# The shared expert's nine-tap convolution by five products for three outputs, with a new order of the lanes and of early preparations

## The chip, the cores and the metric

The kernel runs on one core of one Trainium2 chip. The metric is the device time of one execution in microseconds (us), the median of several runs. In the names of the profile PE is TensorE (PEld its weight loads), DVE VectorE, ACT ScalarE, POOL GpSimd and SP SyncE, which issues DMAs.

## What is computed

An audio tower on x of 8 batches of 750 tokens with 128 channels in float32: layer 0 has a convolution mixer, a gated recurrence and a mixture of 8 experts with a shared one; layer 1 a linear attention over 8 heads and a mixture of 10 experts with a shared convolution. After the mixer's pooling 748 tokens a batch are left. The part that the change rewrites is the shared convolution of layer 1:

```python
xt = jnp.transpose(x, (0, 2, 1))
...
sh = conv1d_same(xt, sh_w1, sh_b1)     # 128 -> 512 channels, 9 taps
sh = jax.nn.silu(sh)
sh = conv1d_same(sh, sh_w2, sh_b2)     # 512 -> 128 channels, 1 tap
sh = jnp.transpose(sh, (0, 2, 1))
z = residual + y + sh
```

## The kernel before

Each engine has one straight program; semaphores order them, and an engine that waits holds back all that stands behind. The phases are: the mixer of layer 0, its experts, attention with the shared convolution, the experts of layer 1 (208 tiles of rows), and the output sums. Between phases stand barriers.

Attention goes over four pairs of batches (ITERS = 4, LANES = 2). A lane has 25 steps: step 0 and 1 sum the experts' rows, take variance 5 and norm 5 on VectorE (rstd 5 on GpSimd between them), step 2 is norm5T on TensorE, 3 to 7 the projections q0, q1, k0, k1 and v, 8 to 19 six chunks of scores and context, 20 (OUT_STEP) the output projection, 21 norm6T, 22 and 23 the router's convolutions, 24 its scores. `interleaved` (from line 579) writes out the order that all engines share: after each step of a lane it puts in as many parts of the convolution of the pair before (i - 1) as the weights FILL allow. Attention of pair 0 has none of them (`conv` is False); after pair 3 its convolution stands alone, the tail.

The convolution (PARTS, line 549 on; `conv_part` on three engines) takes nine taps as three groups g of three. A half-batch q (375 or so columns) and a quarter m of the 512 channels are one unit. With the minimal form for two outputs and three taps it needs four products a, b, c, d of 192 or 182 columns each for a group, into two PSUM banks, "bc" and "ad", 12 instructions a product pair (a float32 matmul is two instructions). ScalarE copies each bank out (line 1434), VectorE combines (`conv_combine`, lines 2015 to 2019), ScalarE takes silu (1422), TensorE then multiplies four quarters with conv2 for three tiles of tokens ("rows", line 1142), ScalarE copies (1447, 1448) and GpSimd adds them to N (`add_conv_rows`, 2199 to 2203). Rows of half-batch q stand after the first product pair of unit (q + 1, m = 1), and those of half-batch 3 at the end (CONV_END).

GpSimd's program for a pair (`attention`, from line 2228) is: turn(1, i-1), rstd 5 of both lanes (2111), add_b_out, add_b_v, add_b_sh2(1, i-1), scatter of lane 0's rows (12 indirect DMAs, 2130), add_conv_rows(0), scatter of lane 1, add_conv_rows(1), rstd 6 of both lanes, add_conv_rows(2), turn(0, i), add_b_sh2(0, i), add_conv_rows(3). `turn` (2225 to 2227) makes the inputs of the products from the transposed norm 6; `add_b_sh2` adds one bias to N and ln_b to H (2191, 2193); `make_conv_weights` (2209 to 2213) stands in pair 0 only. Its memory for the products is `wreg`; the turned inputs lie in NT.

## Time and profile before

| | us |
|---|---|
| median of 3 runs | 1531.79 (1531.74 to 1535.3) |
| the profiled execution | 1544.43 |
| its span | 1542.6 |
| busy TensorE, VectorE, GpSimd, ScalarE | 1305.9, 1003.6, 699.3, 644.9 |
| attention of pair 0, without convolution | 582.0 to 686.6 |
| pairs 1, 2, 3 | 686.6 to 857.0, to 1022.0, to 1186.6 |
| the tail | 1186.6 to 1267.6 |
| experts of layer 1, output | to 1480, to 1542 |

Times of rows count from the start of the span. A row of the order of time has the start, the length of the merged group, engine, line, operation, what it writes and reads, count, and in brackets how long the engine had been idle and what ended that. The granted clock (PEclk) is a share of 2.4 GHz; 0.50 is TensorE's lower level of 1.2 GHz.

### The profile page before, as it was taken

To read this page: it belongs to the slowest core of one execution; us is meant where nothing else is said; L and a number is where in the kernel's file an instruction comes from. 1 tells how busy PE (TensorE), PEld (TensorE's weight loads), DVE (VectorE), ACT (ScalarE), POOL (GpSimd) and SP (SyncE) were. 2 spreads that over 40 slices of the span, in tenths; PEclk is the share of its full clock that TensorE was granted. 3 is DMA by queue.
4 is the path that set the end of the run, shared out by engine and by line. 5 is a ranking of instruction groups with operands and counts; after the bars stand their busy time and mean duration, and the time that the engine had idled before them with its cause. 6 is when DMAs were issued, how large, how long until landed. Compare 5 with 4: busy or idle time off the path is not lost.

```text
span 1542.6 us, 33397 instructions
## 1 busy us (share of the span) xinstructions
PE 1305.9 (85%) x10360; PEld 1103.2 (72%) x10361; DVE 1003.6 (65%) x3235; ACT 644.9 (42%) x1610; POOL 699.3 (45%) x1055
## 2 busy tenths in 40 slices
PE   6696777787899937778899899988998989999974
PEld 3464646564899935556788778876887989999953
DVE  4467768665466656757863786467663628989946
ACT  1346272523122204335335453445334436666623
POOL 0112556444688853133531444242614526777732
PEclk9697989898999978989999899999998999999987
DMA  6000400003588840010010001000100237777725
GB/s 191 4 21 6 111 27 22 25 21 95 161 266 256 263 170 1 2 42 1 24 61 0 2 14 58 14 1 1 43 1 8 95 97 191 196 194 198 196 88 161
DMA packets 102202, 128.46 MB, mean 83 GB/s; under 512 B 21015, under 2 KB 61181, under 8 KB 101842
## 3 DMA queue, kind: packets, MB, share of 16 engines
q1 hardware_dynamic: 88786, 102.36, 23.1%
q0 software_dynamic: 13312, 24.74, 4.8%
q8 instruction: 62, 1.02, 0.3%
q14 instruction: 42, 0.34, 0.1%
HBM read 96.13 MB, written 34.94 MB: 85 GB/s over the span
## 4 chain that ended last, share of the span: by engine, by line
PE 60%; DVE 15%; issue 7%; DVEq 6%; POOL 5%; ACT 4%; DMA 2%; POOLq 0%; SPq 0%; ACTq 0%
PE psum L980 12%; PE psum L1133 11%; PE psum L989 9%; DVE work L1554 3%; PE psum L1142 3%; PE psum L1047 2%; POOL rows_in L2130 2%; PE psum L1094 2%; PE psum L1072 2%; PE psum L794 2%; PE psum L1191 2%; PE psum L969 2%; PE psum L1018 2%; DVE stats L1537 2%; PE psum L1067 1%
## 5 line engine op out<-in xcount | busy, mean ns | idle before, releaser
L1133 PE MATMUL psum<-NT,wreg 128*128 128x182 f32 (+1 forms) x1536 | 261.6, 326 | 10.2 <-ACT pack L1434 5.1
L1133 PEld LDWEIGHTS psum<-NT,wreg 128*128 128x128 f32 x1536 | 247.9, 192 | 18.9 <-ACT pack L1434 5.9
L2162 POOL DMA_INDIRECT rows_out<-work,expert_row_kept x208 | 206.2, 992 | 79.6 <-issue 41.1
L980 PE MATMUL psum<-work 128*128 128x128 f32 x1664 | 222.7, 277 | 0.9 <-ACT work L1336 0.9
L980 PEld LDWEIGHTS psum<-work 128*128 128x128 f32 x1664 | 203.9, 193 | 1.7 <-issue 0.9
L2111 POOL TENSOR_TENSOR rstd<-var_eps,pack 128x6 f32<-128x6 f32 x40 | 56.5, 1415 | 215.0 <-DVE var_eps L1544 214.9
L1329 ACT ACTIVATE work<-psum,work 128x128 f32<-128x128 f32 x416 | 118.6, 368 | 64.4 <-PE psum L980 64.3
L1876 DVE SCALAR_TENSOR_TENSOR work<-psum,work 128x128 f32<-128x128 f32 x416 | 117.1, 344 | 7.7
L794 PE MATMUL psum<-pack,work 128*128 128x128 f32 (+2 forms) x288 | 51.4, 336 | 82.0 <-DVE work L1554 75.5
L1885 DVE TENSOR_SCALAR work<-psum,expert_row_kept 128x128 f32<-128x128 f32 x208 | 72.8, 350 | 71.8 <-PE psum L969 36.6
L2130 POOL DMA_INDIRECT rows_in<-N,slot_now x96 | 100.5, 1046 | 28.6 <-issue 28.4
L989 PE MATMUL psum<-work 128*128 x832 | 110.2, 275 | 1.4 <-DVE work L1876 1.4
L794 PEld LDWEIGHTS psum<-pack,work 128*128 128x128 f32 (+2 forms) x288 | 42.2, 176 | 91.4 <-DVE work L1554 57.3
L989 PEld LDWEIGHTS psum<-work 128*128 128x128 f32 x832 | 101.2, 192 | 2.0 <-issue 2.0
L1322 ACT ACTIVATE work<-psum 128x256 f32<-128x256 f32 x104 | 39.9, 383 | 124.1 <-PE psum L980 116.6
L1047 PE MATMUL psum<-work 64*128 64x256 f32 (+1 forms) x384 | 56.5, 414 | 17.6 <-DVE work L1961 14.7
L1934 DVE TENSOR_TENSOR work<-psum,pack 128x1024 f32<-128x1024 f32 (+1 forms) x48 | 56.5, 1192 | 21.9 <-PE psum L1049 20.6
L1142 PE MATMUL psum<-wreg,conv_h 128*128 128x128 f32 (+1 forms) x384 | 55.4, 311 | 14.5 <-ACT conv_h L1422 14.5
L2199 POOL TENSOR_TENSOR slots_seen<-pack 128x1 f32<-128x1 f32 x16 | 3.1, 191 | 140.5 <-ACT conv_rows L1448 129.5
L969 PE MATMUL psum<-pack,work 128*128 128x128 f32 x208 | 58.7, 283 | 8.2 <-DMA work<-rows_in 5.6
L1142 PEld LDWEIGHTS psum<-wreg,conv_h 128*128 128x128 f32 (+1 forms) x384 | 53.7, 222 | 15.0 <-ACT conv_h L1422 15.0
L989 PE MATMUL psum<-wreg,work 128*128 x416 | 63.6, 276 | 0.8 <-DVE work L1864 0.8
(364 smaller groups left out, 2894.3 us busy)
## 6 DMA issues: line engine op xcount, KB each, us to landing
work<-w_and_b SPq DMA_DIRECT2D x104, 258.0 KB
work<-in_ew SPq DMA_DIRECT2D x104, 256.0 KB
work<-rows_in SPq DMA_DIRECT2D x208, 65.0 KB
work<-rows_out SPq DMA_DIRECT2D x32, 384.0 KB, 4.2
rows_out<-work,expert_row_kept POOLq DMA_INDIRECT x208
work<-in_xT SPq DMA_DIRECT2D x8, 375.0 KB, 3.0
w_and_b<-in_ew SPq DMA_DIRECT2D x1, 2560.0 KB
out<-H SPq DMA_DIRECT2D x8, 320.0 KB
```

The source lines that it names most:

```text
L794: r = nc.tensor.transpose((acc or v.P)[:, j // 3, c0:c0 + widths[j]], src(j), ident[0:widths[j], 0:widths[j]])
L969: nc.tensor.transpose(v.psx, v.x, ident).then_inc(pe_done[k], pe.step(phase, "xT", k))
L980: r_ = mm(v.ps1[:, c * P:(c + 1) * P], v.w1[:, c * P:(c + 1) * P], v.xT, start=True, stop=True)
L989: r_ = mm(v.psy, v.e[:, c * P:(c + 1) * P], weights[:, bass.ds(which[u] * nh + c * P, P)], start=(c == 0), stop=(m == 0 and c == nh - 1))
L1047: mm(acc[:, :, 0:n], v.QK[2 + g][rows, col], v.QB[rows, g, :, 0:n], start=True, stop=True)
L1133: r = mm(bank[:, half * HALF_PAIRS:half * HALF_PAIRS + p1 - p0], weights[:, m * P:(m + 1) * P], product_input(name, g, k, p0, p1), start=( ...
L1142: r = mm(acc, conv_h[:, m, j * P:j * P + n_], conv2[:, m * P:(m + 1) * P], start=(m == 0), stop=(m == 3))
L1329: r_ = A(v.e[:, c * P:(c + 1) * P], v.ps1[:, c * P:(c + 1) * P], ACT.Exp, bias=v.b1[:, c:c + 1])
L1876: r_ = V.scalar_tensor_tensor(v.e[:, cols], v.ps1[:, cols], v.b1[:, c:c + 1], v.e[:, cols], ALU.add, ALU.max)
L1885: V.tensor_scalar(v.y, v.psy, v.gate, None, ALU.mult).then_inc(dve_done[k], dve.step(phase, "y", k))
L2130: G.indirect_dma_start(rows_in[m], bass.IndirectOffsetOnAxis(ap=slot_now[0:n, q, j:j + 1], axis=0), staged(m, q, k)[0:n, j % TILES, :], No ...
L2162: G.indirect_dma_start(rows_out[m], bass.IndirectOffsetOnAxis(ap=v.dest, axis=0), v.y, None, bounds_check=last, oob_is_err=False).then_inc ...
```

## The change

The convolution takes the minimal form for three outputs and three taps: five products (points 0, 1, 2, 3, 4) of 250 columns over a whole batch k, in fills p12, p03 (12 instructions each) and p4 (6), alternating between two banks. A unit is now a batch and a quarter m, eight in a pair in place of sixteen. The weights of two points are made on GpSimd, in eight adds of 1536 columns where there were three; `turn` makes the five inputs in one add of 504 and eleven of 252 columns with three drains between, in place of three of 754. VectorE combines in seven instructions of 250 columns. The quarters m = 2, 3 of the silu input lie in the first two batches of H, which are stored to DRAM before and loaded back during the experts of layer 1; copies of p03 and p4 have one buffer, those of p12 two. Rows of half-batches 0 and 1 come after unit (1, 0), those of 2 and 3 both at the end. ln_b's add is a step of its own (`add_ln_b`), for both lanes right behind turn(0). `interleaved` spreads the parts by COST; without convolution lane 1 goes a step behind lane 0 from step 2 to 7. On VectorE variance 5 and norm 5 of lane 1 are one step, and the router's taps and the route's constants are made before it waits for the row stores. GpSimd's order of steps is not changed otherwise.

```diff
+TRIPLES = (L + 2) // 3
+TURNED = TRIPLES + 2
...
+        CONV_POINTS = 5
+        conv_w = wreg[:, 0:CONV_POINTS * 3 * 512].rearrange("p (x g c) -> p x g c", x=CONV_POINTS, g=3)
+        conv2 = wreg[:, CONV_POINTS * 3 * 512:CONV_POINTS * 3 * 512 + 512]
...
+        conv_h_own = sb("conv_h", [P, 2, TILES * P])
+        conv_h = [conv_h_own[:, m, :] for m in range(2)] + [
+            H[:, m * TILES:(m + 1) * TILES, :].rearrange("p j d -> p (j d)") for m in range(2)]
+        first_rows = H[:, 0:LANES * TILES, :].rearrange("p j d -> p (j d)")
...
+        conv_sum = NTf[:, SUM_AT:SUM_AT + TRIPLES]
+        conv_p12 = [pack[:, PACK[at][0]:PACK[at][0] + 2 * TRIPLES] for at in ("compress", "Wg")]
+        conv_p034 = sb("conv_p034", [P, 3 * TRIPLES])
+        conv_p03, conv_p4 = conv_p034[:, 0:2 * TRIPLES], conv_p034[:, 2 * TRIPLES:]
...
-        UNIT = [(q, m) for q in range(UNITS) for m in range(4)]
+        UNIT = [(k, m) for k in range(LANES) for m in range(4)]
+        POINTS = {"p12": (1, 2), "p03": (0, 3), "p4": (4,)}
 
 
         PARTS = []
-        for u, (q, m) in enumerate(UNIT):
-            PARTS.append(("bc", q, m))
-            if m == 1 and q > 0:
-                PARTS.append(("rows", q - 1, 0))
-            PARTS.append(("ad", q, m))
-        CONV_END = [("last", UNITS - 1, 3), ("rows", UNITS - 1, 0)]
+        for k, m in UNIT:
+            PARTS += [(x, k, m) for x in POINTS]
+            if m == 0 and k > 0:
+                PARTS += [("rows", 2 * k - 2, 0), ("rows", 2 * k - 1, 0)]
+        CONV_END = [("last", LANES - 1, 3), ("rows", UNITS - 2, 0), ("rows", UNITS - 1, 0)]
+        COST = {"p12": 6, "p03": 6, "p4": 3, "rows": 4}
+        FILLS = [f"{x}{m}_{k}" for x, k, m in PARTS + CONV_END if x != "last"]
...
+            costs = [COST[x] for x, *_ in PARTS]
+            turns_ = [(x // LANES, x % LANES) for x in range(ATT_STEPS * LANES)]
+            if not conv:
+                ahead = [x for x in turns_ if x[0] < CHUNKS]
+                ahead.sort(key=lambda x: (x[0] + (x[1] if x[0] > 1 else 0), x[1]))
+                turns_ = ahead + turns_[len(ahead):]
+            for step, lane_ in turns_:
+                order.append(("attention", step, lane_))
+                reached += FILL[step]
+                while conv and n < len(PARTS) and sum(costs[:n]) * sum(FILL) * LANES < reached * sum(costs):
                     order.append(("conv", n, 0))
                     n += 1
...
+            for t, x in enumerate((0, 1, 4)):
+                sp.dma_start(conv_w[:, x], d["conv1"].rearrange("p (g t c) -> p g t c", g=3, t=3)[:, :, t, :]).then_inc(conv_in, 16)
+            sp.dma_start(conv2, d["conv2"]).then_inc(conv_in, 16)
...
+            sp.wait_ge(first_rows_final, 1)
+            sp.dma_start(first_rows_dram, first_rows).then_inc(first_rows_out, 16)
...
+            sp.wait_ge(pe_conv_done, pe_conv.end("conv")[0][1])
+            sp.wait_ge(first_rows_out, 16)
+            sp.dma_start(first_rows, first_rows_dram).then_inc(first_rows_back, 16)
...
+                fill = f"{what}{m}_{k}"
+                bank = fill_bank(fill)
+                before, bi = fill_before(fill, i)
+                e.wait_ge(act_conv_done, act_conv.at("conv", before, 0, bi))
...
+                    if what == "p12" and m == 0:
                         e.wait_ge(pool_done[k], pool.at("attention", "turned", k, i))
-                    e.wait_ge(act_conv_done, act_conv.at("conv", f"{what}{bm}_{bq}", 0, bi))
-                    if what == "ad" and m == 1 and q > 0:
-                        e.wait_ge(act_conv_done, act_conv.at("conv", f"rows{q - 1}", 0, i))
-                    elif what == "ad" and m == 0 and q == 0:
...
+                bk, bm, bi = unit_before(k, m, i, 2 if what == "p12" else 1)
+                e.wait_ge(dve_conv_done, dve_conv.at("conv", f"y{bm}_{bk}", 0, bi))
+                dst = {"p12": conv_p12[u % 2], "p03": conv_p03, "p4": conv_p4}[what]
+                nc.scalar.copy(dst, bank[:, 0:len(POINTS[what]) * TRIPLES]).then_inc(act_conv_done, act_conv.step("conv", fill, 0))
+                if what == "p03" and u > 0:
+                    conv_silu(*UNIT[u - 1], i)
...
             def second_step(k, i):
-                (norm5 if k == 0 else var5)(k, i)
-
-            def third_step(k, i):
                 if k > 0:
-                    norm5(k, i)
-
-            att = {0: [begin_lane], 1: [second_step], 2: [third_step]}
+                    var5(k, i)
+                norm5(k, i)
+
+            att = {0: [begin_lane], 1: [second_step]}
...
+                if u == 2:
+                    e.wait_ge(first_rows_out, 16)
+                e.wait_ge(act_conv_done, act_conv.at("conv", f"p4{m}_{k}", 0, i))
+                V.scalar_tensor_tensor(conv_sum, p1, 3.0, p2, ALU.mult, ALU.add)
+                V.scalar_tensor_tensor(p2, p1, -3.0, p2, ALU.mult, ALU.add)
+                V.scalar_tensor_tensor(p0, p0, 3.0, p3, ALU.mult, ALU.add)
+                V.scalar_tensor_tensor(conv_p4, conv_p4, 1.5, p3, ALU.mult, ALU.add)
                 e.drain()
-                V.scalar_tensor_tensor(y[:, 0], conv_sum[:, 0:n_], 0.5, a, ALU.mult, ALU.add)
-                V.scalar_tensor_tensor(y[:, 1], b, 0.5, d_, ALU.mult, ALU.subtract
-                                       ).then_inc(dve_conv_done, dve_conv.step("conv", f"y{m}_{q}", 0))
+                V.tensor_tensor(y[:, 0], p0, conv_sum, ALU.subtract)
+                V.scalar_tensor_tensor(y[:, 1], p3, 2.0, p2, ALU.mult, ALU.add)
+                V.scalar_tensor_tensor(y[:, 2], conv_p4, 4.0, conv_sum, ALU.mult, ALU.subtract
+                                       ).then_inc(dve_conv_done, dve_conv.step("conv", f"y{m}_{k}", 0))
...
+            def add_ln_b(k, i, first):
+                e.drain()
+                e.wait_ge(dve_done[k], dve.at("attention", "norm6", k, i))
+                G.tensor_tensor(slots_seen[:], w("nought"), w("nought"), ALU.add)
                 for h, n, tiles in tile_halves(H[:, batch_tiles(i * LANES + k), :]):
-                    G.tensor_tensor(h, h, w("ln_b")[0:n].unsqueeze(1).broadcast_to([n, tiles, P]), ALU.add)
+                    r = G.tensor_tensor(h, h, w("ln_b")[0:n].unsqueeze(1).broadcast_to([n, tiles, P]), ALU.add)
+                if first and k == LANES - 1:
+                    r.then_inc(first_rows_final, 1)
...
+                s = N[:, LANES * TILES:2 * LANES * TILES, :].rearrange("p j d -> p (j d)").rearrange("p (g c) -> p g c", g=3)
+                w0, w1, w2, w3, w4 = (conv_w[:, x] for x in range(CONV_POINTS))
+                e.wait_ge(conv_in, 64)
+                G.tensor_tensor(s, w0, w4, ALU.add)
+                G.tensor_tensor(w3, w1, w1, ALU.add)
                 e.drain()
-                G.tensor_tensor(conv_c, s, conv_taps[:, :, 1], ALU.subtract)
+                G.tensor_tensor(w2, s, w1, ALU.subtract)
+                G.tensor_tensor(w3, w3, w0, ALU.add)
                 e.drain()
-                G.tensor_tensor(conv_taps[:, :, 1], conv_taps[:, :, 1], s, ALU.add)
+                G.tensor_tensor(w1, w1, s, ALU.add)
+                e.drain()
+                G.tensor_tensor(s, w4, w4, ALU.add)
+                e.drain()
+                G.tensor_tensor(s, s, s, ALU.add)
+                e.drain()
+                G.tensor_tensor(w3, w3, s, ALU.add)
                 e.drain().then_inc(conv_made, 1)
...
+                    v = NTf[:, at:at + 3 * TURNED].rearrange("p (r s) -> p s r", s=3)
+                    return v[:, 0:n] if n > 1 else v[:, 0]
+
+                G.tensor_tensor(t[:, 3:5], x(3, 2), x(1, 2), ALU.subtract)
+                G.tensor_tensor(t[:, 0], x(0), x(2), ALU.subtract)
+                G.tensor_tensor(t[:, 1], x(1), x(2), ALU.add)
+                G.tensor_tensor(t[:, 2], x(1), x(2), ALU.subtract)
+                e.drain()
+                G.tensor_tensor(t[:, 0], t[:, 0], t[:, 0], ALU.add)
+                G.tensor_tensor(t[:, 1], t[:, 3], t[:, 1], ALU.subtract)
+                G.tensor_tensor(t[:, 2], t[:, 2], t[:, 2], ALU.add)
+                G.tensor_tensor(t[:, 4], t[:, 4], t[:, 3], ALU.subtract)
+                e.drain()
+                G.tensor_tensor(t[:, 0], t[:, 0], t[:, 3], ALU.add)
+                G.tensor_tensor(t[:, 2], t[:, 2], x(3), ALU.add)
+                G.tensor_tensor(t[:, 4], t[:, 4], t[:, 3], ALU.subtract)
+                e.drain()
+                G.tensor_tensor(t[:, 2], t[:, 2], x(2), ALU.subtract
                                 ).then_inc(pool_done[k], pool.step("attention", "turned", k))
...
                 if not first:
                     add_conv_rows(2, i - 1)
                 turn(0, i)
+                add_ln_b(0, i, first)
+                add_ln_b(1, i, first)
                 add_b_sh2(0, i)
                 if not first:
                     add_conv_rows(3, i - 1)
```

## Rows read from the trace of the kernel before

**Rows 1.** The stretches, each engine's busy time and TensorE's granted clock.

```profile
core 0: us, PE busy (x) PEld busy (x) DVE busy (x) ACT busy (x) POOL busy (x), PEclk, DMA share, GB/s
...
857.00:1022.00 165.00, 152.66 (x1372) 128.76 (x1373) 106.59 (x297) 77.08 (x172) 61.66 (x71) 0.96 0.06 21
```

**Rows 2.** The same stretches, the convolution's matmuls of line 1133 alone.

```profile
857.00:1022.00 165.00, 66.18 (x392) 62.18 (x393) 0.96 0.06 21
...
1186.60:1267.60 81.00, 62.58 (x384) 61.16 (x384) 0.97 0.29 93
```

**Rows 3.** TensorE in order of time, the tail after the last batch pair.

```profile
1193.28 15.68 PE L1133 MATMUL psum<-NT,wreg 128*128 128x192 f32 x96
1208.80 2.84 PE L1142 MATMUL psum<-wreg,conv_h 128*128 128x128 f32 x24
...
1262.19 4.56 PE L1142 MATMUL psum<-wreg,conv_h 128*128 128x128 f32 x24 [2.56 <-ACT conv_h L1422]
```

**Rows 4.** TensorE in order of time, from one out projection past the boundary.

```profile
798.16 1.60 PE L1086 MATMUL psum<-pack,work 128*128 128x128 f32 x12
799.60 2.82 PE L1142 MATMUL psum<-wreg,conv_h 128*128 128x128 f32 x24
...
816.52 0.86 PE L794 MATMUL psum<-pack,work 128*128 128x128 f32 x6
...
851.41 5.27 PE L1142 MATMUL psum<-wreg,conv_h 128*128 128x128 f32 x24 [3.98 <-ACT conv_h L1422]
...
857.20 15.87 PE L1133 MATMUL psum<-NT,wreg 128*128 128x192 f32 x96 [0.51 <-issue]
...
877.29 9.66 PE L1018 MATMUL psum<-work,pack 128*128 128x384 f32 x24
```

**Rows 5.** GpSimd in order of time, first conv rows, scatter, rstd6 of pair 1.

```profile
766.93 0.19 POOL L2199 TENSOR_TENSOR slots_seen<-pack 128x1 f32<-128x1 f32 x1 [2.09 <-issue]
...
768.39 0.33 POOL L2125 TENSOR_TENSOR slots_seen<-pack 128x1 f32<-128x1 f32 x1 [0.17 <-issue]
769.09 0.99 POOL L2130 DMA_INDIRECT rows_in<-wreg,slot_now  x1 [0.37 <-issue]
...
783.24 0.99 POOL L2130 DMA_INDIRECT rows_in<-work,slot_now  x1 [0.30 <-issue]
...
804.71 1.47 POOL L2111 TENSOR_TENSOR rstd<-var_eps,pack 128x6 f32<-128x6 f32 x1
```

**Rows 6.** GpSimd in order of time, at the boundary between two pairs.

```profile
848.55 2.21 POOL L2191 TENSOR_TENSOR N<-N,row_bias 128x640 f32 x2 [17.17 <-ACT work L1403]
850.73 1.68 POOL L2193 TENSOR_TENSOR H<-H,pack 128x640 f32 x2
...
859.45 1.44 POOL L2225 TENSOR_TENSOR NT<-NT 128x754 f32<-128x754 f32 x1
```

**Rows 7.** GpSimd in order of time, the weights' preparation in pair 0.

```profile
618.05 3.45 POOL L2211 TENSOR_TENSOR wreg<-conv_h,wreg 128x1536 f32<-128x1536 f32 x1 [8.64 <-issue]
621.65 3.41 POOL L2213 TENSOR_TENSOR wreg<-wreg,conv_h 128x1536 f32<-128x1536 f32 x1 [0.15 <-issue]
```

**Rows 8.** VectorE in order of time, pair 0 and the start of pair 1.

```profile
565.95 1.02 DVE L1895 MEMSET work<- 128x1152 f32 x1 [9.66 <-DMA rows_out<-work,expert_row_kept]
...
621.85 3.36 DVE L1957 TENSOR_TENSOR work<-work,upd 128x128 f32<-128x128 f32 x1
...
688.20 8.21 DVE L1916 TENSOR_TENSOR H<-work,H 128x640 f32 x2 [0.20 <-issue]
...
704.59 1.63 DVE L1554 TENSOR_SCALAR work<-H,mean_var,rstd 128x128 f32 x6 [0.18 <-issue]
...
709.73 2.99 DVE L1554 TENSOR_SCALAR work<-H,mean_var,rstd 128x128 f32 x6 [0.25 <-POOL rstd L2111]
```

**Rows 9.** TensorE in order of time, pair 0.

```profile
585.51 1.51 PE L794 MATMUL psum<-pack,work 128*128 128x128 f32 x6 [4.85 <-DVE work L1554]
...
626.59 2.08 PE L1047 MATMUL psum<-work 64*128 64x256 f32 x8 [5.77 <-DVE work L1961]
```

More of the change, by code:

```diff
@@ L1145, in none @@
+                r.then_inc(pe_conv_done, pe_conv.step("conv", fill, 0))
             def none(k, i):
@@ new lines, in conv_silu @@
+            def conv_silu(k, m, i):
+                e.wait_ge(dve_conv_done, dve_conv.at("conv", f"y{m}_{k}", 0, i))
+                A(conv_h[m][:, 0:L], conv_h[m][:, 0:L], ACT.Silu, bias=w("b_sh1", (m, m + 1)), scale=1.0 / 6.0
+                  ).then_inc(act_conv_done, act_conv.step("conv", f"s{m}_{k}", 0))
+            def conv_part(n, i):
+                what, k, m = (PARTS + CONV_END)[n]
+                u = 4 * k + m
+                if what == "last":
+                    conv_silu(k, m, i)
+                    return
+                fill = f"{what}{m}_{k}"
+                bank = fill_bank(fill)
+                e.wait_ge(pe_conv_done, pe_conv.at("conv", fill, 0, i))
+                if what == "rows":
+                    q = k
@@ L2021, in conv_combine @@
                 e.drain()
             def conv_part(n, i):
[L2024 to L2027 removed]
+                what, k, m = (PARTS + CONV_END)[n]
+                if what == "p12" and 4 * k + m > 0:
+                    conv_combine(*UNIT[4 * k + m - 1], i)
                 elif what == "last":
[L2029 removed]
+                    conv_combine(k, m, i)
```

190 lines of the change are left out of this document (75 added, 115 removed).

## The prediction

> **Names.** Eight batches run in pairs: pair 0 to pair 3 of the attention loop, two lanes (0 and 1) in a pair. A pair's convolution is done while the next pair's attention runs; that of the last pair is the tail. Rows_q are the pointwise products of half-batch q (24 instructions of line 1142), a fill is one group of convolution products between two bank changes. All engines run their programs in order.
>
> **What bounds the kernel now.** I read the stretches first, then TensorE's own order of time, then GpSimd's. In a pair's stretch of 165.0 us TensorE is busy 152.7, VectorE 106.6, GpSimd 61.7 [rows 1]: TensorE is the bound, and 66.2 us of it are the products of line 1133, 62.6 in the tail [rows 2]. So work taken from TensorE there is worth its length, as long as nothing else comes late. The reader is to see a second thing: GpSimd is idle most of the time, but it is one queue, and TensorE waits through it: for rstd (line 2111), for the turned inputs (2225 to 2227). What stands ahead of these in GpSimd's program matters, not its busy share.
>
> **The gain on TensorE.** Per pair the old form needs 384 instructions of 192 or 182 columns (two for each matmul call), the new one 2 batches x 4 m x 15 calls x 2 = 240 of 250 columns. 96 old ones took 15.68 us, 0.163 each, and 24 of 128 columns 2.84, 0.118 [rows 3]. Through both points 250 columns cost 0.204, in proportion to columns 0.212; I take 0.212, since 0.163 for 192 is nearly in proportion. A pair is then 50.9 us against 62.6, or 54 against 66 at a pair's mean clock: **12 us less** in each of four places, 47 in all. Against this stands the order of the work.
>
> **First wait: rstd6 behind the scatter.** Counting the fills of `interleaved` with the new costs (8 units of 15 plus 8, total 128): at step OUT_STEP of lane 0 the fraction reached is 25.5/39 or 83.7, so rows_0 and rows_1 (ending at 79 and 83) come only right after out of lane 0; before, rows_0 came in chunk 1 and only rows_1 stood there, at 799.60 [rows 4]. GpSimd's program is unchanged there: rows_0, scatter of lane 1, rows_1, rstd6. Before, that scatter ran from 769.09 to 784.23 and was over when rows_1 came [rows 5]. Now it starts after rows_0. From rows_0's end on TensorE to norm6 of lane 0: ScalarE's copy 0.7, the add 1.5 (766.93 to 768.39), to the first issue 0.7, twelve issues 15.1, the gap behind them 2.1, rows_1 1.5, rstd 1.5 [rows 5], norm6 1.6 [rows 8]: 24.7 us. TensorE has beside it rows_1 2.8, three fills of 2.5, 2.5 and 1.3, and out of lane 1 1.5 [rows 3, 4]: 10.7. **It waits 14 us**, in pairs 1 to 3, and stands before norm6T (816.52 in pair 1 [rows 4]).
>
> **Second wait: the turned inputs behind rows_2.** Rows_2 moves from inside the pair to its end (CONV_END), behind the last silu, and GpSimd adds it before `turn(0)`. Before, turn(0) was long done when the pair ended. Now the next pair's first fill waits for: copy 0.7, the add 1.5, turn. Turn is new too: one add of 504 and eleven of 252 columns and three drains in place of three of 754 at 1.44 [rows 6]. By that row's 1.91 ns a column it is 6.3 + 0.5 = 6.8 us; by 2.25 ns of the 1536-column adds (3.45 [rows 7]) and the 0.19 that one column costs [rows 5] 10.2. I take 8.5. So the first fill starts 11 us after rows_2's end; rows_3 (2.8 to 5.3) is all that lies beside it.
>
> **Third wait: rstd5 behind two turns.** After turn(0) GpSimd has add_ln_b twice (1.68 and a gate each, 2.1; before one of them stood here, now both do), b_sh2 2.2 [rows 6], rows_3 1.5, turn(1) 8.5, rstd5 1.5. With the 11 that is 28.9 us after rows_2's end, 30.6 with norm5 of lane 0. The fills ahead of it are 54 instructions, 11.4 us, done at about 24 with the slow clock below. From the start of norm5 of lane 0 to the end of that of lane 1 the kernel before takes 8.1 us (704.59 to 712.72 [rows 8]); only now there is no fill between. So q0 starts 5.3 (rows_2) + 38.5 = 43.8 us after rows_2's start, where before it was 877.29 - 851.41 = 25.9 after rows_3's start [rows 4], with 96 of 384 instructions done against 54 of 240.
>
> **A cycle of pairs 2 and 3**, from the last rows' start: q0 at 43.8. From q0 to out of lane 0 the old cycle has 165.0 - 79.1 = 85.9 us [rows 1, 4]; the fills in it fall from 132 instructions at 0.172 (66.2/384 [rows 2]), 22.7, and one rows group to 96 at 0.212, 20.4, of which I count 4 of the 5 us, since VectorE's combine grows from four to seven instructions. Out at 125.7, rows_0's end at 130.0, norm6T at 154.7. From norm6T to the last rows the old pair has 34.9 us with 84 instructions (14.2), one rows group (2.8) and 4.0 idle [rows 4]; the new one 60 instructions (12.7), no rows group, 4.7 idle for the longer combine and silu and 2.5 for the clock: 33.8. The cycle is 188.5, **23.6 over** the 164.9 of before, twice: **+47.2**.
>
> **The clock.** After 4.0 us without work rows_3 took 5.27 for what is 2.82 at the full clock [rows 4]: TensorE ran at the lower of its two levels, 1.2 in place of 2.4 GHz. Each new long gap costs about 2.5 so; I put it behind the two gaps above and in the tail, and one more rows group lies at the end.
>
> **Pair 1.** At its start no rows stand before the turns. Turn(1) and b_sh2 lie as before and the longer turn ends about where the old one with ln_b did, so q0 is taken as before (2 less to 3 more). Then -4 in the chunks, 24.7 + 4.3 from out to norm6T in place of 18.4 [rows 4], 33.8 in place of 34.9: **+5.6**.
>
> **The tail** from rows_2's start: 5.3 + 11 + 50.9 + two rows groups 5.7 + 3 (clock; one late combine behind the slots) + 4.7 idle + rows_2 and rows_3 8.5 (24 took 4.56 in the old tail [rows 3]) = 89.1; before 5.3 + 80.2 (1186.6 to 1266.8 [rows 2, 3]): **+3.7**. The scatter ends at about 71 and the first expert rows come before TensorE is free, so the later scatter costs nothing; it would cost its excess over 18 us. The 8-unit order needs turn(1) at 44 us, it ends at 33.
>
> **Pair 0.** The weights' preparation grows from three adds of 1536 columns to eight, 3.4 us each [rows 7]. While one ran, a 0.29 us add of VectorE took 3.36 and ended with it, and TensorE stood 5.77 [rows 8, 9]. The old three cost about 7 us (three VectorE instructions stretched so), in proportion the five new ones 12; I take +12, with the bounds +4 (most of them meet nothing) and 5 x 3.4 = +17 (each holds VectorE for its whole length). The Trainium skill, "SBUF — State Buffer", section "Who interferes with whom", states that a VectorE instruction with two SBUF inputs and a GpSimd instruction that reads SBUF exclude each other for a whole instruction. By it the upper bound would hold wherever VectorE has such an instruction next, and the longer turns would hold it back too, so the rule speaks against this change; the trace agrees for the one add (621.85 + 3.36 against 621.65 + 3.41). VectorE's preparations before the row stores: it waited 9.66 there [rows 8], so they are hidden, but the loads of Y land about as late: -1.5 (0 to -2.2). The step between lanes: TensorE was idle 4.85 before norm5T of lane 1 [rows 9], but lane 1's chain starts no sooner: -1.5 (0 to -4.9). Sum **+9**. The store and reload of first rows (768 KB) run on SP's queue beside compute; it stands ahead of loads due a pair later, and is over before combine 2 asks: 0.
>
> **Sum.** 9 + 5.6 + 47.2 + 3.7 = +65.5 on the profiled execution of 1544.4. That is 0.8% above the median of the runs, so +65 on 1531.8: **1597 us**.
>
> **Rivals.** (a) The forecast, 0.68. (b) VectorE and GpSimd block each other more: combine 0 and h3 fall into turn(1) (two adds took 8.21 us beside GpSimd [rows 8]), 4 us a boundary, weights at +17: +15, 1612; for it speaks that the boundary now has 25 us of GpSimd without a pause; 0.12. (c) Small turns are cheap, 4.3 us as the old: two turns less a cycle and one in the tail, 4.2 x 5 = -21: 1576; against it speak the fixed part of each instruction and the drains; 0.10. (d) Faster: TensorE's columns alone decide. -47, +9 for pair 0, +12 for rows at the lower clock and longer ends: 1506. It decides if norm6 follows rows_0 within 10.7 us and turn(0) rows_2 within 5; twelve issues alone are 15.1, so I give it 0.06. (e) The waits and the gain cancel, within 0.3%: 0.04 (a measurement of this kernel can tell 0.3% from no change).
>
> **Range and chances.** (a) spans 1570 to 1622 by its bounds: pair 0 +3 to +15, turns 6.8 to 10.2 in five places. The range 1565 to 1625 takes in (c) and (b). Faster 0.06, same 0.04, slower 0.90.
>
> **What would show it.** TensorE idle about 14 us before line 794's norm6T, released by VectorE, with GpSimd's twelve issues between the first two adds of conv rows; the first fill released by GpSimd's turn, 11 us after rows_2; norm5T late by 5 to 10 us; conv matmuls of 0.21 us and four groups of about 52 us; adds of 1536 columns x8 in pair 0. A granted clock below 0.95 in pairs 2 and 3. Wrong would be: rstd6 ahead of the scatter, or turn under 5 us.

## The result, and the profile after

| | before | changed |
|---|---|---|
| median, us | 1532.2 (1531.7 to 1535.3, 4 runs) | 1619.1 (1612.5 to 1623.4, 4 runs) |
| profiled execution, its span | 1544.4, 1542.6 | 1612.5, 1610.5 |
| ratio of the times | 1 | 1.056 [1.051, 1.061] |
| busy TensorE, VectorE, GpSimd | 1305.9, 1003.6, 699.3 | 1266.6, 997.0, 749.8 |

The changed kernel is 87 us slower. The direction is as forecast (1597, range 1565 to 1625), and the time is 22 us above the predicted time. TensorE is busy 39 us less and the kernel takes longer, so the loss is all waiting. TensorE's waits in the changed kernel (line waited in, what released it; total, times, longest):

```profile
PE psum L827 <- DVE work L1586: 140.6, 22, 24.5
PE psum L1174 <- POOL NT L2289: 26.8, 3, 9.4
...
PE psum L1167 <- ACT H L1454: 18.8, 5, 4.7
```

Line 827 is the transposes (794 before), 1174 the convolution (1133), 1167 the rows (1142), 2289 the last instruction of the turn. The same pair in TensorE's order of time, beside [rows 4]:

```profile
859.58 1.23 PE L1167 MATMUL psum<-wreg,conv_h 128*128 128x128 f32 x4 [4.74 <-ACT H L1454]
...
876.23 13.57 PE L1174 MATMUL psum<-NT,wreg 128*128 128x250 f32 x54 [9.39 <-POOL NT L2289]
896.17 1.51 PE L827 MATMUL psum<-pack,work 128*128 128x128 f32 x6 [6.37 <-DVE work L1586]
902.59 1.51 PE L827 MATMUL psum<-pack,work 128*128 128x128 f32 x6 [4.91 <-DVE work L1586]
...
1016.91 1.51 PE L827 MATMUL psum<-pack,work 128*128 128x128 f32 x6 [14.37 <-DVE work L1586]
...
1050.61 1.22 PE L1167 MATMUL psum<-wreg,conv_h 128*128 128x128 f32 x4 [4.74 <-ACT H L1454]
```

From one pair's last rows to the next pair's are 191.0 us, where before there were 163.6 and 166.3. In them TensorE is idle 48.1 us (12.3 before): the first fill waits for the turn, norm5T for both lanes' norms, norm6T for rstd6. GpSimd at the same boundary, to be read beside [rows 6]:

```profile
864.91 0.19 POOL L2239 TENSOR_TENSOR slots_seen<-pack 128x1 f32<-128x1 f32 x1 [39.19 <-ACT conv_rows L1472]
...
866.15 1.03 POOL L2275 TENSOR_TENSOR NT<-NT 128x504 f32<-128x504 f32 x1
...
875.40 0.78 POOL L2289 TENSOR_TENSOR NT<-NT 128x252 f32<-128x252 f32 x1
876.40 0.19 POOL L2229 TENSOR_TENSOR slots_seen<-pack 128x1 f32<-128x1 f32 x1 [0.22 <-issue]
...
882.34 0.19 POOL L2239 TENSOR_TENSOR slots_seen<-pack 128x1 f32<-128x1 f32 x1 [0.21 <-issue]
...
883.58 1.04 POOL L2275 TENSOR_TENSOR NT<-NT 128x504 f32<-128x504 f32 x1
...
893.12 1.33 POOL L2144 TENSOR_TENSOR rstd<-var_eps,pack 128x6 f32<-128x6 f32 x1
```

GpSimd stood idle 39 us waiting for rows_2, while turn(0)'s inputs were complete from 828.5 on (ScalarE's copy of norm6T), 36 us earlier, and then worked 29.5 us almost without a pause, with rstd5 at the end of it. The row with 39.19 in brackets is the cause of the wait for the turn. The cause of the wait at norm6T is in GpSimd's rows between the adds of rows_0 and rows_1, to be read beside [rows 5]:

```profile
992.96 0.19 POOL L2239 TENSOR_TENSOR slots_seen<-pack 128x1 f32<-128x1 f32 x1 [35.11 <-ACT conv_rows L1472]
...
995.12 1.18 POOL L2163 DMA_INDIRECT rows_in<-NT,slot_now  x1 [0.52 <-issue]
...
1012.60 0.19 POOL L2239 TENSOR_TENSOR slots_seen<-pack 128x1 f32<-128x1 f32 x1 [2.16 <-issue]
...
1013.83 2.66 POOL L2144 TENSOR_TENSOR rstd<-var_eps,pack 128x6 f32<-128x6 f32 x2
```

The twelve issues stand between the two adds, and both rstd6 behind them; VectorE had waited 13.15 us for them when it began norm6.

### The profile page after: what moved, and what is told of

The parts are those of the page before. It is cut to its first block, busy times and chain, and to the rows that moved or that the text cites. A ratio compares the mean times of both kernels' runs of the same rounds, so it can differ in the third digit from the quotient of the medians.

```text
span 1610.5 us, 32139 instructions
## 1 busy us (share of the span) xinstructions
PE 1266.6 (79%) x9784; PEld 1042.6 (65%) x9785; DVE 997.0 (62%) x3204; ACT 620.0 (38%) x1540; POOL 749.8 (47%) x1140
## 3 DMA queue, kind: packets, MB, share of 16 engines
q1 hardware_dynamic: 90130, 103.93, 22.7%
## 4 chain that ended last, share of the span: by engine, by line
PE 40%; issue 22%; DVE 13%; POOL 12%; ACT 4%; DVEq 3%; POOLq 3%; DMA 2%; SPq 0%; ACTq 0%
PE psum L1013 11%; PE psum L1022 8%; POOL rows_in L2163 6%; PE psum L1174 4%; DVE work L1586 2%; PE psum L1224 2%; PE psum L1002 2%; PE psum L827 2%; PE psum L1051 1%; POOL rstd L2144 1%; DVE stats L1569 1%; PE psum L845 1%; PE psum L1080 1%; PE psum L846 1%; POOLq L2237 1%
## 5 line engine op out<-in xcount | busy, mean ns | idle before, releaser
L1174 PE MATMUL psum<-NT,wreg 128*128 128x250 f32 x960 | 224.9, 390 | 30.2 <-POOL NT L2289 26.8
L1174 PEld LDWEIGHTS psum<-NT,wreg 128*128 128x128 f32 x960 | 186.6, 199 | 56.6 <-POOL NT L2289 19.1
L827 PE MATMUL psum<-pack,work 128*128 128x128 f32 (+2 forms) x288 | 56.9, 361 | 146.9 <-DVE work L1586 140.6
L827 PEld LDWEIGHTS psum<-pack,work 128*128 128x128 f32 (+2 forms) x288 | 46.7, 191 | 158.5 <-DVE work L1586 124.1
L1022 PE MATMUL psum<-work 128*128 x832 | 110.2, 275 | 1.8 <-DVE work L1908 1.8
L2045 DVE SCALAR_TENSOR_TENSOR NT<-pack 128x250 f32<-128x250 f32 x32 | 15.6, 487 | 104.1 <-ACT conv_p L1478 94.1
L1586 DVE TENSOR_SCALAR work<-H,mean_var,rstd 128x128 f32 (+1 forms) x96 | 31.4, 397 | 51.4 <-POOL rstd L2144 50.8
```

What stands on the lines that cost most here:

```text
L827: r = nc.tensor.transpose((acc or v.P)[:, j // 3, c0:c0 + widths[j]], src(j), ident[0:widths[j], 0:widths[j]])
L1022: r_ = mm(v.psy, v.e[:, c * P:(c + 1) * P], weights[:, bass.ds(which[u] * nh + c * P, P)], start=(c == 0), stop=(m == 0 and c == nh - 1))
L1174: r = mm(bank[:, half * TRIPLES:(half + 1) * TRIPLES], conv_w[:, x, g, k_cols(m)], turned(k)[:, x, g:g + TRIPLES], start=(g == 0), stop=(g ...
```

## The experiments

All times of one table row come from one chip, and each ratio is to the kernel before on that chip, since the chips differ. "Cycle" is the time from the last rows of pair 1 to those of pair 3, halved, read in the trace. The kernel before has one trace only, that of its profile above; its cycle does not come from the group on A. On which chip the first comparison ran is not known; the changed kernel was not run again on A or B.

| kernel | chip | median | ratio to before | cycle |
|---|---|---|---|---|
| before | A | 1533.0 | 1 | 164.9 (trace of its profile) |
| changed (first comparison, before 1532.2) | | 1619.1 | 1.056 [1.051, 1.061] | 191.1 |
| e1: rows_2 behind turn(0) | A | 1588.0 | 1.037 [1.033, 1.041] | 181.8 |
| e2: rstd6 ahead of the rows | A | 1583.1 | 1.034 [1.030, 1.038] | 181.1 |
| e3: both | A | 1559.2 | 1.016 [1.012, 1.020] | 172.4 |
| e4: both, rstd5 ahead of turn(1) | A | 1570.9 | 1.023 [1.019, 1.027] | 176.1 |
| before | B | 1667.3 | 1 | |
| e5: both, turn(0) behind norm6 | B | 1660.3 | 0.996 [0.993, 0.998] | 188.4 |
| e6: changed, three weights' adds | B | 1704.9 | 1.025 [1.021, 1.029] | 207.0 |
| e7: before with the small parts | B | 1681.4 | 1.009 [1.006, 1.012] | 193.1 |
| e8: before with a long turn | B | 1692.2 | 1.013 [1.010, 1.017] | 193.9 |
| before | C | 1652.7 | 1 | |
| e9: changed | C | 1698.6 | 1.028 [1.023, 1.033] | 206.5 |
| e10: as e3 | C | 1671.4 | 1.011 [1.006, 1.016] | 196.2 |
| e11: as e5 | C | 1644.8 | 0.994 [0.990, 0.997] | 187.7 |
| e12: e5 and norm5 ahead | C | 1628.1 | 0.986 [0.982, 0.990] | 180.5 |

### Are the two waits in GpSimd's queue the loss? (e1, e2, e3)

e1 changes the end of GpSimd's `attention`, e2 its middle:

```diff
-                if not first:
-                    add_conv_rows(2, i - 1)
                 turn(0, i)
                 add_ln_b(0, i, first)
                 add_ln_b(1, i, first)
                 add_b_sh2(0, i)
                 if not first:
+                    add_conv_rows(2, i - 1)
                     add_conv_rows(3, i - 1)
```

```diff
                     scatter(1, i - 1, [0])
-                    add_conv_rows(0, i - 1)
                     scatter(1, i - 1, [1])
-                    add_conv_rows(1, i - 1)
                 for k in range(LANES):
                     rstd("attention", 6, k, i)
+                if not first:
+                    add_conv_rows(0, i - 1)
+                    add_conv_rows(1, i - 1)
```

> The changed kernel, with GpSimd's add of the third convolution rows (add_conv_rows(2)) moved behind turn(0), both add_ln_b and add_b_sh2(0), just ahead of add_conv_rows(3). Same instructions on every engine, only GpSimd's order differs. Theory (GpSimd's queue at the boundary of the pairs): turn(0) no longer waits for TensorE's third rows, so the 9.4 us wait of the first fill goes in pairs 1 to 2 and in the tail (8.1 us), and norm5 of the next pair starts some 8 to 10 us sooner, since turn(0), ln_b and b_sh2(0) are done ahead of the rows: 2 x 14 to 18 + 8 = 36 to 44 us less than the changed kernel, about 1578 against 1619. Rival 1 (VectorE and GpSimd stand in each other's way, and that is the cost): the same work overlaps, so less than 10 us go. Rival 2 (the order hides a third wait that takes its place, norm5's rstd behind turn(1)): only the fill's 27 us go.

> The changed kernel, with GpSimd's rstd6 of both lanes moved ahead of add_conv_rows(0) and (1), and the second half of the scatter ahead of them too; nothing else differs. Theory (rstd6 behind the scatter behind the first rows): TensorE's wait of 14.4 us at norm6 in each of pairs 1 to 3 goes, 43 us less in all, about 1576 against 1619; what is next late is VectorE's own norm6, some 3 us of each may stay, so 34 to 43. Rival 1 (contention of VectorE and GpSimd): under 10 us go. Rival 2 (the scatter itself, 12 indirect DMA a lane at about 1.3 us each, is what rstd6 waits for, not the rows): half of it stays.

> Both moves of GpSimd's queue together, nothing else. Theory: the two waits are in different places of a pair and add up: 36 to 44 and 34 to 43 us, so 70 to 87 less than the changed kernel, 1532 to 1549, about the kernel before. Rival (the convolution's work is in part the cover of what follows, or contention is the cost): less than 50 us go, above 1569.

Measured against the changed kernel's 1619: -31, -36 and -60 us, each good to about 9 us. The 1619 come from the first comparison and not from the group on A, but the kernel before took 1532.2 there and 1533.0 on A; on chip C, where the changed kernel and the one with both moves ran together (e9, e10), the two moves give back 27 of 46 us. Both rivals of pure contention (under 10 us) fall: with not one instruction changed, an order gives back 60 of the 87 us. The cycles add up: -9.3, -10.0, together -18.7. e1's 31 lie between the 27 of its rival 2 and the 36 of the theory. The third wait did not take the place of the first, as that rival had it: from the last rows to q0 are 13.6 us less, and norm5T of lane 0 waits 0.2 in place of 6.4 in pair 2; but 3.1 are lost again between norm6T and the next last rows. e1's waits, in the form of the first list, no longer hold the one for the turn, and the tail, which waited for its first turn too, is 12.3 us shorter (85.0 to 72.7 to the start of the last rows). The line for the silu grew by 4.5; turn(0) and add_b_sh2(0) now lie beside the last combine:

```profile
PE psum L827 <- DVE work L1586: 133.6, 24, 25.0
PE psum L1080 <- DVE work L1998: 25.5, 18, 6.6
PE psum L1167 <- ACT H L1454: 23.3, 5, 6.3
```

e2's line for the norms fell from 140.6 to 106.8, 11 us a pair, and not 14: norm6T still waits 1.1 and 2.2 for VectorE. Both scatters still stand ahead of rstd6, so they were not the reason by themselves, as rival 2 of e2 had it: they cost only where the second started behind rows_0. In e3 the norms' line stands at 107.8, but one wait at norm6T is back:

```profile
991.76 0.86 PE L827 MATMUL psum<-pack,work 128*128 128x128 f32 x6 [1.10 <-DVE work L1586]
...
1001.04 1.51 PE L827 MATMUL psum<-pack,work 128*128 128x128 f32 x6 [5.87 <-DVE work L1586]
```

e1 and e3 came out under what was expected and e2 near its lower end: each time a part of the gain met the next wait.

### The third wait (e4)

```diff
-                if not first:
-                    turn(1, i - 1)
                 for k in range(LANES):
                     rstd("attention", 5, k, i)
+                if not first:
+                    turn(1, i - 1)
```

> Both moves, and the third wait as well: GpSimd does rstd5 of both lanes ahead of turn(1) at the start of a pair (the turned columns get a semaphore of their own so that this order can be said). Theory: norm5 of lane 0 no longer waits for turn(1)'s 9.6 us where that is not already covered: 5 to 10 us less in each of pairs 1 to 3 beside the two moves, 15 to 30 in all: 1505 to 1530, at or below the kernel before (1532). Rival: norm5 then waits for VectorE's var5 behind its combine of the convolution, and nothing more goes (within 5 us of the kernel with both moves).

The rival is right, and worse than it said: 12 us slower than e3 in the median (four runs each, 1561.9 to 1572.8 against 1552.6 to 1565.1), and 3.7 in the cycle. GpSimd gives rstd5 sooner, but VectorE's program has the first combine of the convolution ahead of norm5, and it waits for ScalarE's copy of p4. In e3 already:

```profile
878.66 0.49 DVE L2045 SCALAR_TENSOR_TENSOR NT<-pack 128x250 f32<-128x250 f32 x1 [7.65 <-ACT conv_p L1478]
...
882.74 1.63 DVE L1586 TENSOR_SCALAR work<-H,mean_var,rstd 128x128 f32 x6 [0.18 <-issue]
```

In e3 turn(1) lay beside these 7.65 us of an idle VectorE. In e4 GpSimd stands still there instead, for var5 of lane 1, which VectorE does behind the combine and norm5 of lane 0. Turn(1) then comes from 885.2 to 893.9, and add_b_out behind it beside the route's count, whose first copy takes 1.26 us where it takes 0.22 in e3:

```profile
883.90 1.33 POOL L2148 TENSOR_TENSOR rstd<-var_eps,pack 128x6 f32<-128x6 f32 x1 [11.42 <-DVE var_eps L1578]
885.20 1.03 POOL L2279 TENSOR_TENSOR NT<-NT 128x504 f32<-128x504 f32 x1
...
893.89 4.59 POOL L2213 TENSOR_TENSOR H<-H,row_bias 128x640 f32 x4
```

TensorE has a new wait there (9.1 us over three pairs), and from norm5T to norm6T of lane 1 are 115.2 us in place of 110.2:

```profile
PE psum L938 <- DVE N L1710: 9.1, 3, 3.4
```

### Contention of VectorE and GpSimd (e5, e11)

```diff
                 else:
+                    add_b_sh2(0, i - 1)
                     add_b_sh2(1, i - 1)
...
                 for k in range(LANES):
                     rstd("attention", 6, k, i)
+                add_ln_b(1, i, first)
+                add_ln_b(0, i, first)
                 if not first:
                     add_conv_rows(0, i - 1)
                     add_conv_rows(1, i - 1)
                 turn(0, i)
-                add_ln_b(0, i, first)
-                add_ln_b(1, i, first)
-                add_b_sh2(0, i)
```

> The kernel with both moves, and GpSimd's order changed once more, with no instruction added or taken: add_ln_b(1) and add_ln_b(0) (which wait for norm6) go ahead of the adds of the first two rows and of turn(0), and add_b_sh2(0) goes to the next pair, beside add_b_sh2(1). In the trace of the kernel with both moves norm6 of lane 1 took 5.81 us for six instructions beside turn(0), where six alone took 1.63. Theory of contention between VectorE and GpSimd: with GpSimd idle there those six take about 1.6 again, TensorE's 5.87 us wait at norm6 of lane 1 falls to about 1.7, and the last combine ahead of the last rows loses some 1.3: 4 to 6 us a pair, 12 to 18 in all: 1541 to 1547 against 1559. Rival (what bounds there is something else, the six are only stretched because nobody waits for them): no difference beyond 3 us.

> The kernel whose turn(0) waits until norm6 of lane 1 is over, again, now beside the kernel with both moves. Its trace has all of norm6's instructions at 0.33 to 0.35 us, where up to 3.19 us stood beside the turn. Theory of contention: 0.008 to 0.012 below the ratio of the kernel with both moves (12 to 18 us). Rival (the stretched instructions lay in slack): within 0.003 of it, and the gain seen came from the chip.

The six instructions of norm6 of lane 1 in e3, beside turn(0), and in e5, with GpSimd idle:

```profile
995.17 5.81 DVE L1586 TENSOR_SCALAR work<-H,mean_var,rstd 128x128 f32 x6
```

```profile
1067.41 1.63 DVE L1586 TENSOR_SCALAR work<-H,mean_var,rstd 128x128 f32 x6
```

TensorE's wait behind them falls from 5.87 to 0.94, and that for the silu ahead of the last rows from 6.25 to 4.74. e5 ran on chip B, where e3 did not, so its whole time decides nothing. On chip C, where both ran, e11 is 0.017 below e10, 27 us, with intervals that do not touch. The slack theory falls. The size is larger than the 12 to 18 expected. The two cycles give 8.5 each, 17.0, and norm5T to the last rows in pair 1 another 7.9. At the end of pair 0, where turn(1) had stood behind both add_ln_b and add_b_sh2(0), come about 5 more: norm5T of lane 1 is 8.3 us earlier, of which 3.3 were there when attention began. Since add_b_sh2(0) and add_ln_b were moved too, the whole 27 us is not contention's: the two waits above are 6.4 us a pair (the six instructions alone 4.2), and what the moved adds bring by themselves no run took apart.

### Pair 0 and the small parts (e6, e7)

e6 makes three adds in `make_conv_weights` and leaves out five, so its output differs. e7 puts into the kernel before this, and VectorE's early preparations:

```diff
+            if not conv:
+                ahead = [x for x in turns_ if x[0] < CHUNKS]
+                ahead.sort(key=lambda x: (x[0] + (x[1] if x[0] > 1 else 0), x[1]))
+                turns_ = ahead + turns_[len(ahead):]
...
-                (norm5 if k == 0 else var5)(k, i)
+                if k > 0:
+                    var5(k, i)
+                norm5(k, i)
```

> The changed kernel with three of the eight adds that make the convolution's weights (the kernel before had three); the other weights are left out, so the output differs, and nothing else does. Theory: pair 0 is longer by these adds, each about 3 us of GpSimd beside VectorE's work, which stretches VectorE's instructions: 6 to 12 us less than the changed kernel, 1607 to 1613 against 1619. Rival (they lie in idle time): no difference; and the 6 us by which pair 0 grew come from elsewhere.

> The kernel before with the two small parts of the change alone: lane 1 a step behind lane 0 up to the first chunks in pair 0, and VectorE's early preparations with var5 and norm5 of lane 1 in one step. No new convolution. Theory of the sum: 3 us less in pair 0 (1.5 and 1.5), nothing elsewhere: 1528 to 1532 against 1533. Rival 1 (the merged step puts norm5 of lane 1 directly behind its own variance, with rstd5's round trip through GpSimd uncovered): 2 to 3 us more in each pair, 1537 to 1541. Rival 2: nothing that can be measured.

The whole time of e6 can't be set beside the changed kernel's, which ran on another chip (1.025 against 1.028 on C). Its trace can: from norm5T of lane 0 to norm6T in pair 0 are 91.0 us in e6, 97.0 in e9, 96.9 in the changed kernel's first trace and 90.0 in that of before. So five adds are 6.0 us, 1.2 each, and not the 12 of the forecast; the gain is at the lower end of the 6 to 12 expected, and the rival falls.

e7 came out 15 us slower than before (10 to 20), where 3 less were forecast. Pair 0 gained nothing: 90.6 us in that stretch against 90.3 in e8, which has the old step order, and the wait before it 22.7 against 22.9. What the traces show of the loss is at the start of pairs 1 to 3, where q0's first product now waits:

```profile
939.76 1.51 PE L799 MATMUL psum<-pack,work 128*128 128x128 f32 x6 [2.94 <-DVE work L1559]
943.81 2.86 PE L1023 MATMUL psum<-work,pack 128*128 128x384 f32 x4 [2.54 <-ACT work L1360]
```

In [rows 4] q0 follows norm5T without a wait. So it does in e8, on the same chip and with the old steps. The three such waits (3.2, 2.5 and 2.9) are 8.7 us; for the rest of the 15 there is no trace of before on chip B, and it stays open. Rival 1 had the place right and the size at half.

### The turn's length alone (e8)

```diff
+                for again in range(2):
+                    G.tensor_tensor(t[:, 0, :, 0:n], x(0), x(2), ALU.subtract)
+                    G.tensor_tensor(t[:, 1, :, 0:n], x(1), x(2), ALU.add)
+                    G.tensor_tensor(t[:, 2, :, 0:n], x(2), x(1), ALU.subtract)
+                    e.drain()
```

> The kernel before with a turn of eight instructions instead of three (the first three repeated and repeated again in part, with the same results), about 11.5 us instead of 4.3; the convolution is the old one. Theory (queue): turn(0) stays hidden, since in this kernel only the last rows stand at the pair's end and turn(0) is not behind them; turn(1) holds rstd5 back, so norm5 of lane 0 comes about 5 us later at each boundary: 10 to 20 us more, 1543 to 1553. That is far from the 87 us of the whole change: what costs is the order in which the rows, the turn and rstd stand, not the turn's length. Rival (the turn's work beside VectorE costs by itself): 7 us twice a pair, 30 us or more.

Measured +22 us (16 to 28), just above the theory's 10 to 20 and under the rival's 30. The turn has nine instructions, not the eight that I had counted, and took 14.6 us beside VectorE's work (930.77 to 945.41), so turn(1) is 10 longer, twice the 4 to 6 by which the change lengthens it. The 22 us cannot be set beside the 87, since the kernel before took 1532 us in that comparison and 1667 on B: on B the changed kernel without five of its adds (e6) is 42 us slower than before, so about 48 with them. Halved for the shorter turn, e8 leaves it some 11 us of that, an estimate: a longer turn costs some, and the 9.3 and 10.0 us a cycle that e1 and e2 gave back by order alone are more. The trace shows what the turn does to VectorE:

```profile
930.82 4.22 DVE L1544 TENSOR_SCALAR var_eps<-mean_var 128x6 f32<-128x6 f32 x1
...
936.09 3.24 DVE L1916 TENSOR_TENSOR H<-work,H 128x640 f32 x2 [0.20 <-issue]
```

The first takes 0.17 and the second 1.03 with GpSimd idle.

### A version that beats both (e9, e10, e12)

e12 takes e5, puts rstd5 ahead of turn(1) as e4, and clears VectorE's way too (the separate wait in norm5_kept stands for what the combine had implied, that ScalarE has read norm 6):

```diff
-        FILL = [3, 1, 0, 0, 0, 0, 1, 0] + [0.5, 0.5] * TILES + [3.5, 2, 1.5, 1, 0.5]
+        FILL = [2, 0, 2, 0, 0, 0, 1, 0] + [0.5, 0.5] * TILES + [3.5, 2, 1.5, 1, 0.5]
...
                 add_experts(k, i)
-                if k == 0:
-                    var5(k, i)
+                var5(k, i)
...
-            att = {0: [begin_lane], 1: [second_step]}
+            def norm5_kept(k, i):
+                e.wait_ge(act_done[k], act.at("attention", "kept", k, i - 1))
+                norm5(k, i)
+
+            att = {0: [begin_lane], 1: [norm5_kept]}
```

> The changed kernel itself once more, as the reference of this group on one chip, since the chip of the last group gave the kernel before 1667 us where the chip of the group before it gave 1533. Expected from its first comparison: 1.056 times the kernel before on a chip like the first. On a chip like the second, where TensorE stands idle at many single instructions with nothing awaited, the changed kernel has 576 TensorE instructions fewer, so the ratio may be lower, 1.03 to 1.05.

> The kernel with both moves of GpSimd's queue again, beside the next one on the same chip. Expected: 1.016 times the kernel before on a chip like the first, and 0.035 to 0.045 below the changed kernel's ratio on any chip, since the two waits do not depend on it.

> The same, and the pair's boundary in another order on VectorE and GpSimd: var5 of both lanes in the first step, norm5 of both lanes in the second, with fewer of the convolution's fills ahead of them and more behind norm5's transposes (2, 0, 2 in place of 3, 1, 0 of the planner's dues), so that no combine stands ahead of norm5; GpSimd's rstd5 of both lanes goes ahead of turn(1). Theory (after the queue's waits and the contention, what is left over the kernel before is norm5 behind the first combine, with a 5.6 us wait of TensorE at norm5 of lane 1 and 1 at lane 0): 5 to 7 us a pair less, 15 to 21 in all, so the ratio falls by another 0.010 to 0.014, to 0.99 or below. Rival 1 (as rstd5 ahead of turn(1) alone brought nothing and cost 12: turn(1) then stands beside VectorE's work of the first chunks): no gain or a loss. Rival 2 (the fills that came ahead of norm5 were its cover): TensorE waits at norm5 of lane 0 instead, and half of the gain stays.

e12 is 1.4% faster than the kernel before and 4.2% faster than the changed one on the same chip. Its boundary has no wait at norm5T:

```profile
897.36 1.22 PE L1169 MATMUL psum<-wreg,conv_h 128*128 128x128 f32 x4 [4.74 <-ACT H L1456]
...
907.85 6.59 PE L1176 MATMUL psum<-NT,wreg 128*128 128x250 f32 x30 [2.11 <-issue]
914.28 0.81 PE L829 MATMUL psum<-pack,work 128*128 128x128 f32 x6
914.92 2.71 PE L1176 MATMUL psum<-NT,wreg 128*128 128x250 f32 x12
917.47 0.80 PE L829 MATMUL psum<-pack,work 128*128 128x128 f32 x6
```

What cost 3.7 us a cycle alone in e4 brings 7.2 with its partner on VectorE. That both engines on the way to norm5 had to be cleared at once is argued: VectorE's new order was not run with GpSimd's old one. The ratio fell by 0.008, a little less than the 0.010 to 0.014 expected.

e9 fell as expected or a little more (1.028, where 1.03 to 1.05 stood), but e10 lies only 0.018 below it, 29 us, and not 0.035 to 0.045. The waits did go as on A. But on C TensorE loses time with nothing awaited (its row has "issue" in brackets), and more of it in e10: idle so per cycle 6.6 us in e9 and 13.9 in e10, where the first traces of the two kernels show none and 1.8. Busy and clock of these two cycles, e9 and then e10, beside those of the changed kernel's and e3's first traces:

```profile
905.10:1110.70 205.60, 152.54 (x1220) 118.19 (x1220) 101.14 (x278) 68.82 (x151) 68.60 (x88) 0.85 0.05 16
```

```profile
912.20:1108.70 196.50, 156.26 (x1220) 118.78 (x1220) 104.47 (x278) 68.98 (x151) 68.39 (x88) 0.88 0.05 17
```

```profile
859.60:1050.60 191.00, 142.93 (x1220) 113.21 (x1220) 101.53 (x278) 68.99 (x151) 68.90 (x88) 0.88 0.06 18
```

```profile
861.50:1034.50 173.00, 143.98 (x1221) 113.89 (x1221) 104.16 (x278) 68.98 (x151) 68.78 (x88) 0.92 0.06 19
```

So on C each cycle is 15 to 24 us longer with the same instructions: 7 and 12 of it are this idle time, and 10 and 12 are TensorE's busy time, which is longer too, at a granted clock of 0.85 and 0.88 in place of 0.88 and 0.92. And the expectation that the gain of an order is the same on any chip was wrong. What holds TensorE there is open: no run took it apart.

## Why the prediction was right, and where it was off

| step | forecast | traces |
|---|---|---|
| wait at norm6T of lane 0 | 14 | 14.4 |
| turn | 8.5 (6.8 to 10.2) | 8.6 alone, 10.0 and 9.6 beside VectorE |
| q0 after the last rows' start | 43.8 | 44.3 |
| a matmul of 250 columns | 0.212 | 0.22 (13.23 for 60) |
| cycle of pairs 2 and 3 | 188.5 | 191.1 |
| pairs 2 and 3 | +47.2 | +52.3 |
| pair 1 | +5.6 | +7.4 |
| tail | +3.7 | +6.7 |
| pair 0 | +9 | +6.0 |
| sum of these | +65.5 | +72.4 |

**The mechanism.** All three waits stand where they were forecast, with the releasers named, and e1, e2 and e3 show that the first two carry most of the loss: 60 us of 87 go by order alone. Between the turns and q0 the parts were off more than their sum: the two turns took 19.6 us in place of 17, and q0 came at 44.3 in place of 43.8.

**The cycles.** 2.6 us each were missed. Of these 2.2 lie between q0 and out of lane 0, where the sum took the old 85.9 less 4. TensorE's busy time fell there by 5.1 as reckoned (80.9, the mean of the two old pairs, to 75.8), but its idle time rose from 4.8 to 8.3, where the sum had given the longer combine 1 us. The mis-sized term is this one. The longest of these waits, 3.41, is behind VectorE's count for the route, where before a rows group lay beside it; the others were not taken apart. The fill after the second wait took 13.57 for 54 instructions, where 11.4 stood in the sum, at a granted clock of 0.85, but that cost nothing: it was over at 889.8, and norm5T stood until 896.2 for VectorE. The granted clock of the whole cycle is 0.88, against 0.96 before. Of the 47 us forecast as the gain on the matmuls 36.7 came in busy time (224.9 against 261.6 in the three pairs and the tail).

**Pair 0.** Nearer in sum (9 for 6.0) than in its terms, by luck: two errors had opposite signs. The weights were +12 and measured 6.0 (e6), and the two small gains of 1.5 were not there (e7 against e8). The step that failed is "in proportion the five new ones 12". Beside the three old adds VectorE lost 6.9 us in three places (1.99 and 2.77 for what takes 0.48, 3.36 for 0.29), as reckoned. Beside the eight of the changed kernel it lost 13.2 in four (4.40, 5.58 and 2.22 for 0.48, 2.69 for 0.29): the last two adds met nothing that was stretched. That is 6.3 more, and TensorE's waits for VectorE in these chunks rose by as little, from 8.8 to 13.9 us. The rule of the Trainium skill, "SBUF — State Buffer", section "Who interferes with whom", as the forecast put it, speaks of an instruction of VectorE with two inputs in SBUF. In the changed kernel's trace such instructions were stretched where they met GpSimd's adds (1.47 for 0.41 us at the boundary), but the upper bound that the forecast drew from it did not come. Norm 6's instructions in e3 have one such tensor, and were stretched as well (5.81 for 1.63). How often the two engines meet is a matter of the order, and that I did not work out. e7's loss in the later pairs was in no term at all: I had costed var5 and norm5 in one step at nothing there.

**The median.** The sum was made on one execution and carried over to the median as it stood. In spans the change is +67.9, in medians +86.9. The difference is 12.2 us by which the profiled execution of before lay above its median, and 6.6 by which the changed kernel's lay below. Part of it is the work ahead of attention: six traces with nearly the same program up to there begin norm5T between 571.6 and 579.2 us, that of before at 579.2 and that of the changed kernel at 574.0. The forecast said that the profiled execution was 0.8% above the median and then let it cancel; it does so only if the other kernel's is as high. Of the 22 us by which 1597 fell short, 7 are the terms above and 15 this. So 1619 fell in the range by its width: the range also took in (b) and (c). The bounds that the forecast names for (a), pair 0 at +3 to +15 and five turns of 6.8 to 10.2, give 1582 to 1612 and not the 1570 to 1622 written there, and 1619 lies above them.

**The rivals.** (b), contention, had the place and the size of a stretch at the boundary right: the first combine took 6.5 us beside turn(1) and 2.7 alone, 3.8 where 4 were named. But in the changed kernel that cost nothing, since VectorE then waited 2.76 more for rstd5:

```profile
885.18 1.47 DVE L2045 SCALAR_TENSOR_TENSOR NT<-pack 128x250 f32<-128x250 f32 x1 [15.05 <-ACT conv_p L1478]
...
894.49 1.63 DVE L1586 TENSOR_SCALAR work<-H,mean_var,rstd 128x128 f32 x6 [2.76 <-POOL rstd L2144]
```

What contention cost there is the 2.4 us by which the two turns together were longer than two alone. (b) was wrong for the weights. Its 1612 lies nearer to the result than 1597, but for the reason just told. (c) cheap turns and (d) columns alone fell by the table. (d)'s point, that the columns would decide if the order let them, e12 bears out in part: it is 1.4% faster than before on C, where (d) had 1.7% for the change as it stood.

## What to carry to other kernels

When work moves to the end of a stage on one engine, look at every queue in which its consumer stands: here an add of 1.3 us held back a turn whose inputs had been ready for 36 us, and that held back the next stage's norm. Order a shared helper queue by the time at which each step's input is ready and its result is needed, and look at all engines on the way together, since one cleared alone may show a loss, as in e4. Put the helper's long stretches beside times when VectorE is idle.

## What the runs showed of the hardware

- Short instructions of VectorE took far longer beside GpSimd's adds. In e8 a write of 128x6 took 4.22 us beside three adds of 1.44 us, ending with the third, and 0.17 alone, and norm's six TENSOR_SCALAR, with one tensor read from SBUF each, took 5.81 in e3 against 1.63 in e5. GpSimd's adds of 754 columns in turn rose from 1.44 to 2.04 in e8, beside VectorE's two-input adds.
- After 9.4 us of idling the fill of 54 matmuls took 13.57 us at a granted clock of 0.85; the same fill after 1.8 us in e3 took 11.65 at 1.00. The cycles' granted clock went 0.96, 0.92, 0.88 as the idle time in them went up from 12 to 29 and 48 us (before, e3, changed).
- Chips differ. The kernel before took 1533, 1667 and 1653 us on A, B and C. Every trace of B and C has, between 700 and 1300 us, 25 to 66 places where TensorE stood idle for up to 2.1 us with nothing awaited, 20 to 40 us in all; those of the first comparison and of A have three at most, 4 us in all. On C the gain of the two moves was about half (29 us against 60). What makes the difference was not found; the kernel before itself has no trace on B or C.
